# Root and rows of the norm on GpSimd, statistics in other units, and four of six low parts on VectorE, in a kernel of linear attention and experts

## The reference

```python
xn = layernorm(x)
# attention: 16 heads of 16, 128 random features a head
q, k, v = split(xn @ W_qkv.T)
q_p = elu(q @ proj) + 1 ; k_p = elu(k @ proj) + 1
kv = k_p.T @ v
attn = (q_p @ kv) / (q_p @ k_p.sum(tokens) + 1e-8)
# experts: 8 of 256 -> 1024 -> 256, the two best of each token
logits = xn @ Wr + br ; weights = softmax over the top 2
ffn = sum_e weights_e * (gelu(xn @ W1_e + b1_e) @ W2_e + b2_e)
out = x + attn @ W_out.T + b_out + ffn
```

## Time and profile before

| | us |
|---|---|
| median of three runs | 700.1 |
| profiled execution | 700.86 |
| its span, first to last instruction | 698.7 |
| TensorE busy | 682.9 |
| VectorE busy | 504.1 |
| ScalarE busy | 475.3 |
| GpSimd busy | 227.9 |

### The profile page before, as it was taken

How to read it: one execution, slowest core, us unless ns; L and a number is a source line. 1 busy time by engine, 2 the same in 40 slices (tenths; PEclk the granted TensorE clock), 3 DMA queues, 4 the chain that set the end, 5 groups by cost and what they waited for, 6 DMA issues and landing times.

```text
span 698.7 us, 17362 instructions
## 1 busy us (share of the span) xinstructions
PE 682.9 (98%) x5503; PEld 603.3 (86%) x5504; DVE 504.1 (72%) x1246; ACT 475.3 (68%) x875; POOL 227.9 (33%) x169
## 2 busy tenths in 40 slices
PE   8899999999999998999999999999999999999996
PEld 4666777777777776589999999999999999999996
DVE  8798888888888878748577675556777545577544
ACT  5687969696969696776557775447775444577553
POOL 2053232323232324643232532225233222322422
PEclk9999999999999999999999999999999999999999
DMA  8856474747474647765455663336556333454531
GB/s 266 200 182 170 108 228 106 228 106 228 106 228 106 198 106 223 224 189 142 100 98 118 145 167 46 46 47 106 178 71 167 48 52 53 81 131 107 69 48 23
DMA packets 87205, 91.65 MB, mean 131 GB/s; under 512 B 60049, under 2 KB 73361, under 8 KB 84897
## 3 DMA queue, kind: packets, MB, share of 16 engines
q1 hardware_dynamic: 71426, 59.36, 33.9%
q0 software_dynamic: 13872, 18.75, 15.2%
q10 hardware_dynamic: 1872, 13.11, 5.1%
HBM read 39.32 MB, written 26.67 MB: 94 GB/s over the span
## 4 chain that ended last, share of the span: by engine, by line
PE 82%; DVE 6%; issue 4%; ACT 2%; POOL 2%; DMA 2%; SPq 1%; POOLq 0%; DVEq 0%
PE F L527 9%; PE F L528 9%; PE F L529 9%; PE WK L527 5%; PE F L596 5%; PE WK L529 4%; PE WK L528 4%; PE NUM L527 4%; PE NUM L529 4%; PE NUM L528 4%; PE DEN L605 4%; PE DEN L527 4%; PE DEN L529 4%; PE DEN L528 4%; PE F L590 3%
## 5 line engine op out<-in xcount | busy, mean ns | idle before, releaser
L1932 POOL DMA_INDIRECT out<-ysb,icur x75 | 121.0, 1613 | 270.6 <-DVE ysb L1763 241.0
L1218 ACT ACTIVATE h<-F,b1c 128x384 f32<-128x384 f32 x200 | 112.2, 575 | 140.0 <-PE F L529 131.2
L1740 DVE TENSOR_TENSOR hl<-h,hh 128x768 fp32r<-128x768 f32 x100 | 96.1, 962 | 111.6 <-ACT hh L1222 111.6
L1063 ACT ACTIVATE e_ring<-F 128x512 f32<-128x512 f32 x256 | 145.7, 621 | 38.5 <-PE F L590 35.0
L527 PE MATMUL F<-gxh,wh 128*128 128x384 f32 (+1 forms) x400 | 128.6, 321 | 0.4 <-DVE wl L1641 0.4
L528 PE MATMUL F<-gxl,wh 128*128 128x384 f32 (+1 forms) x400 | 128.0, 320 | 0.0
L529 PE MATMUL F<-gxh,wl 128*128 128x384 f32 (+1 forms) x400 | 128.0, 320 | 0.0
L1866 POOL DMA_INDIRECT xg<-rows,slots x64 | 63.2, 988 | 174.0 <-PE F L590 158.8
L1468 DVE SCALAR_TENSOR_TENSOR kp<-F,e_ring 128x512 f32<-128x512 f32 x128 | 82.7, 680 | 13.2 <-PE DEN L605 6.2
L1468 DVE SCALAR_TENSOR_TENSOR qp<-F,e_ring 128x512 f32<-128x512 f32 x128 | 85.2, 683 | 8.5 <-ACT e_ring L1063 7.0
L1222 ACT ACTIVATE hh<-h 128x768 fp32r<-128x768 f32 x100 | 84.6, 846 | 3.3
(11 more groups left out here) (261 smaller groups left out, 1552.6 us busy)
## 6 DMA issues: line engine op xcount, KB each, us to landing
wraw<-experts ACTq DMA_DIRECT2D x12, 1024.0 KB, 6.2
gblk<-xg SPq DMA_DIRECT2D x100, 96.0 KB
Sk<-kdh SPq DMA_DIRECT2D x64, 128.0 KB, 2.3
Sq<-qdh SPq DMA_DIRECT2D x64, 128.0 KB
xin<-x SPq DMA_DIRECT2D x8, 512.0 KB, 5.5
Sk<-kdl SPq DMA_DIRECT2D x32, 128.0 KB, 2.4
Sq<-qdl SPq DMA_DIRECT2D x32, 128.0 KB
xres<-x SPq DMA_DIRECT2D x8, 512.0 KB
```

Of the source, the lines that this page charges most:

```text
L1063: A(e_ring[:, u % 4, :], F[u % 4][:, :], ACT.Exp, bias=EXP_BIAS, scale=1.0 / DOWN).then_inc(exp_done, 1)
L1218: A(h32[:, m, :], F[m % 4][:, 0:T], ACT.Gelu, bias=b1c[:, w, m:m + 1]).then_inc(gelu, 1)
L1740: V.tensor_tensor(hl[:, 2 * q:2 * q + 2, :], h32[:, 2 * q:2 * q + 2, :], f32(hh[:, 2 * q:2 * q + 2, :]), ALU.subtract).then_inc(hl_rdy, 1)
L1932: pool.indirect_dma_start(out, bass.IndirectOffsetOnAxis(icur[:, s, :], 0), ysb[:, s, :], None, bounds_check=last_token, compute_op=ALU.ad ...
```

## The change

- *Root and rows.* VectorE makes statistics, variance and seed. From batch 2 on GpSimd computes the inverse root (`norm_root`: eleven `tensor_tensor` on 128x4 elements, each waiting for the one before) and writes `xn` (`norm_rows`: four `tensor_scalar`). They stand behind the sends: root of batch `b + 2`, copy of the rows of `b + 1`, rows of `xn` for `b + 2`, and then the bias.
- *Next tokens.* SyncE's `load_x(b + 3)` stands between `stack_k(b + 1)` and `stack_q(b + 1)`.
- *Statistics.* From pass 2 on they stand in units 1 and 2 and the variance with the seed in unit 8; in passes 0 and 1 (`late`) they stay in 16 and 17, and variance and seed are together in 18.
- *Low parts.* `qk_rest` and `qk_lo` of groups 0, 1, 2 and `heads_rest` and `at_lo` of group 0 are gone in the loop. VectorE subtracts the high part from the bank instead: `qk_low` ahead of features 12, 17 and 23, `heads_low` ahead of feature 22. Groups 3 and 1 stay as they were, and so does the last batch's end.

```diff
@@ sync
+        load_x(3)
+        with sp.Fori(1, NB - 3) as b:
+            stack_k(b + 1)
+            load_x(b + 3)
+            stack_q(b + 1)
+            store_o(b - 1)
+            load_xres(b)
...
@@ tensor, iteration
                 if u == 11:
                     kv(b, 1)
-                    qk_rest(b + 1, 0)
...
-                if u == 18:
-                    qk_rest(b + 1, 1)
...
                 if u == 21:
-                    if not first:
-                        heads_rest(b - 1, 0)
                     v_logits(b + 1, 1)
                 if u == 23:
-                    qk_rest(b + 1, 2)
                     pe.wait_ge(kv_rdy, b + 1)
                     v_logits(b + 1, 2)
...
@@ scalar, iteration
-                if u == 11:
-                    qk_lo(b + 1, 0)
...
                 if u == 19:
-                    qk_lo(b + 1, 1)
                     v_copy(b + 1, 0)
...
-                    if not first:
-                        at_lo(b - 1, 0)
-                if u == 22:
-                    qk_lo(b + 1, 2)
...
@@ vector
+        def qk_low(b, i):
+
+            dve.wait_ge(qkh_rdy, 4 * b + i + 1)
+            high, low = ((kdh, kdl), (qdh, qdl))[i // 2]
+            V.tensor_tensor(low[:, i % 2, :], QK_BANK[i][:, :], f32(high[:, i % 2, :]), ALU.subtract).then_inc(qkl_rdy, 1)
+
+        def heads_low(b):
+
+            dve.wait_ge(ath_rdy, 2 * b + 1)
+            V.tensor_tensor(atl[:, 0, :], AT_BANK[0][:, :], f32(ath[:, 0, :]), ALU.subtract).then_inc(atl_rdy, 1)
...
-        def iteration(b, first=False, ahead=True):
+        def iteration(b, first=False, ahead=True, late=False):
             for u in range(32):
-                if u == 0 and not first:
-                    norm_rows(b + 1, 0, 4)
+                if ahead and u == (16 if late else 1):
+                    norm_stats(b + 2, 0, 2)
+                if ahead and u == (17 if late else 2):
+                    norm_stats(b + 2, 2, 4)
+                    join()
+                if ahead and u == (18 if late else 8):
+                    norm_var(b + 2)
+                    for i in range(SEED_STEPS):
+                        norm_step(b + 2, i)
...
+                if u == 12:
+                    qk_low(b + 1, 0)
+                if u == 17:
+                    qk_low(b + 1, 1)
+                if u == 22 and not first:
+                    heads_low(b - 1)
+                if u == 23:
+                    qk_low(b + 1, 2)
...
@@ gpsimd
+        def norm_root(b, i):
...
+            pool.wait_ge(seed_rdy, i + 1)
+            G.tensor_tensor(rtmp[:, 0, :], seed, seed, ALU.mult).then_inc(root_step, 1)
+            pool.wait_ge(root_step, ROOT_STEPS * i + 1)
+            G.tensor_tensor(rtmp[:, 1, :], rtmp[:, 0, :], var[:, :], ALU.mult).then_inc(root_step, 1)
...
+        def norm_rows(b, i):
+            pool.wait_ge(root_step, ROOT_STEPS * i + 11)
+            pool.wait_ge(rows_rdy, b)
+            pool.wait_ge(xT_full, KT * b)
+            pool.sem_inc(root_rdy, 1)
+            for n in range(NT):
+                last = nc.gpsimd.tensor_scalar(xn[:, n, :], xin[:, n, :], mv[:, n, 0:1], rs[:, 1, n:n + 1], ALU.subtract, ALU.mult)
+            last.then_inc(xn_rdy, 1)
...
-        with pool.Fori(1, NB - 1) as b:
+        with pool.Fori(1, NB - 2) as b:
             send(b)
+            norm_root(b + 2, b)
+            copy_rows(b + 1)
+            norm_rows(b + 2, b)
             add_bias(b - 1)
-            copy_rows(b + 1)
```

More of the change, by code:

```diff
@@ L53 @@
 C_T, C_LIM, C_OFF = 324, 336, 344
-C_END = C_OFF + E * TT
+C_ROOT = C_OFF + E * TT
+C_END = C_ROOT + 4
+CUBE = 0.375
 def constants():
@@ L245, in build @@
     xn_first = sem("xn_first")
+    seed_rdy = sem("seed_rdy")
+    root_step = sem("root_step")
+    root_rdy = sem("root_rdy")
     xT_full = sem("xT_full")
@@ L320, in build @@
     ROUTE_STEPS = 8
-    NORM_STEPS, CUBE = 9, 0.375
-    STEPS_AT = {19: (0, 1), 21: (2,), 23: (3, 4), 24: (5,), 25: (6,), 26: (7,), 29: (8,)}
+    NORM_STEPS = 9
+    SEED_STEPS, ROOT_STEPS = 2, 11
     PIECES, PIECE = 4, 1024
@@ L437, in _ @@
         stack_q(1)
-        with sp.Fori(1, NB - 2) as b:
-            load_x(b + 2)
+        load_x(3)
[5 more added lines that the diff above has]
+            load_xres(b)
+        for b in (NB - 3, NB - 2):
             stack_k(b + 1)
@@ L443, in _ @@
             load_xres(b)
[L444 to L447, removed]
         load_raw = load_raw_on(sp)
@@ L1040, in qk_lo @@
         def qk_lo(b, i):
-            act.wait_ge(qkr_full, 4 * b + i + 1)
+            act.wait_ge(qkr_full, i + 1 if isinstance(b, int) and b == 0 else 4 + b)
             A((kdl, qdl)[i // 2][:, i % 2, :], QK_BANK[i][:, :], ACT.Copy).then_inc(qkl_rdy, 1)
@@ L1364, in norm_step @@
             elif i == 1:
-                link(V.tensor_scalar(seed.bitcast(I32), var[:, :].bitcast(I32), -0.5, float(0x5F3759DF), ALU.mult, ALU.add))
+                guess = V.tensor_scalar(seed.bitcast(I32), var[:, :].bitcast(I32), -0.5, float(0x5F3759DF), ALU.mult, ALU.add)
+                if isinstance(b, int) and b < 2:
+                    link(guess)
+                else:
+                    guess.then_inc(seed_rdy, 1)
             elif i == 2:
@@ L1726, in _ @@
         before = chain[1] + ROUTE_STEPS
-        iteration(0, first=True)
+        iteration(0, first=True, late=True)
         batch_steps = chain[1] - before
-        with dve.Fori(1, NB - 2) as b:
+        iteration(1, late=True)
+        with dve.Fori(2, NB - 2) as b:
             chain[:] = before + b * batch_steps, 0
@@ L1860, in copy_rows, with constant @@
             nc.gpsimd.tensor_copy(rows[:, :, 0:D], xn[:, :, :]).then_inc(rows_rdy, 1)
+        def norm_root(b, i):
+            G = nc.gpsimd
+            seed, cubic, root = rs[:, 1, :], rs[:, 0, :], rs[:, 1, :]
+            def constant(k):
+                return cst[:, C_ROOT + k:C_ROOT + k + 1].to_broadcast([P, NT])
+            pool.wait_ge(seed_rdy, i + 1)
+            G.tensor_tensor(rtmp[:, 0, :], seed, seed, ALU.mult).then_inc(root_step, 1)
+            pool.wait_ge(root_step, ROOT_STEPS * i + 1)
+            G.tensor_tensor(rtmp[:, 1, :], rtmp[:, 0, :], var[:, :], ALU.mult).then_inc(root_step, 1)
+            pool.wait_ge(root_step, ROOT_STEPS * i + 2)
+            G.tensor_tensor(rtmp[:, 0, :], rtmp[:, 1, :], constant(0), ALU.add).then_inc(root_step, 1)
+            pool.wait_ge(root_step, ROOT_STEPS * i + 3)
+            G.tensor_tensor(rtmp[:, 0, :], rtmp[:, 0, :], rtmp[:, 1, :], ALU.mult).then_inc(root_step, 1)
+            pool.wait_ge(root_step, ROOT_STEPS * i + 4)
+            G.tensor_tensor(rtmp[:, 0, :], rtmp[:, 0, :], constant(1), ALU.add).then_inc(root_step, 1)
+            pool.wait_ge(root_step, ROOT_STEPS * i + 5)
+            G.tensor_tensor(cubic, rtmp[:, 0, :], seed, ALU.mult).then_inc(root_step, 1)
+            pool.wait_ge(root_step, ROOT_STEPS * i + 6)
+            G.tensor_tensor(rtmp[:, 0, :], cubic, cubic, ALU.mult).then_inc(root_step, 1)
+            pool.wait_ge(root_step, ROOT_STEPS * i + 7)
+            G.tensor_tensor(rtmp[:, 1, :], rtmp[:, 0, :], var[:, :], ALU.mult).then_inc(root_step, 1)
+            pool.wait_ge(root_step, ROOT_STEPS * i + 8)
+            G.tensor_tensor(rtmp[:, 0, :], rtmp[:, 1, :], constant(2), ALU.mult).then_inc(root_step, 1)
+            pool.wait_ge(root_step, ROOT_STEPS * i + 9)
+            G.tensor_tensor(rtmp[:, 0, :], rtmp[:, 0, :], constant(3), ALU.add).then_inc(root_step, 1)
+            pool.wait_ge(root_step, ROOT_STEPS * i + 10)
+            G.tensor_tensor(root, rtmp[:, 0, :], cubic, ALU.mult).then_inc(root_step, 1)
@@ L1891, in _ @@
         send(0)
+        norm_root(2, 0)
         copy_rows(1)
-        with pool.Fori(1, NB - 1) as b:
+        norm_rows(2, 0)
+        with pool.Fori(1, NB - 2) as b:
             send(b)
+            norm_root(b + 2, b)
+            copy_rows(b + 1)
+            norm_rows(b + 2, b)
             add_bias(b - 1)
-            copy_rows(b + 1)
+        send(NB - 2)
+        add_bias(NB - 3)
+        copy_rows(NB - 1)
         def split_weights(c):
```

3 lines of the change are left out of this document (2 added, 1 removed).

## The result

The changed kernel takes 704.19 us, the median of five runs (703.19 to 705.06), beside 700.08 (699.58 to 700.13) for the kernel before: a ratio of 1.0054, interval 1.0042 to 1.0065. Its profiled execution took 704.36 us, 702.5 of it span. The forecast was 704.1 us and slower.

The account below looks back on a forecast made before the run. TensorE looked like the bound, but its weight loads of units 26 and 27 already waited for VectorE, so places there decide. Batch 0, batch 1 and the rest, 1.1 + 1.4 + 1.55 = 4.0 us, gave 704.1 us, range 696.9 to 706.5.

Parts of the forecast that it names:

- Units 0 to 11, nothing: Middle pass: moved statistics, and aggregate, variance and seed (0.75 us) before feature 8, lie in VectorE's waits and cost nothing.
- Unit 17, 0.12 late: Middle pass: the first removed matmul gives nothing, and unit 17's weight load waits for VectorE, 0.12 us late.
- Units 18 to 21, 0.12 early: Middle pass: qk_low(1) ends early, the second removed matmul gives its 0.24 us, unit 21 is 0.12 early.
- The row of five on VectorE from feature 21: Middle pass: features 21 to 23 with two subtractions between run back to back; unit 27 and the pass are 0.31 us late.
- Batches 2 to 6: The middle passes, each 0.31 us late: 1.55 us in all.
- Batch 1: Statistics stay late, ahead of qk_low(1): to_heads starts 1.0 us late and unit 27 is 1.4 us late.
- Batch 0: Three new qk_low subtractions, less removed steps and idle time on VectorE, make it 1.1 us longer.
- GpSimd hidden: GpSimd after its sends: root steps, copy, rows and bias take 7.8 of the 15.3 us before the residual needs the bias.
- The lock: SBUF port, locked for a whole instruction: GpSimd's new work can meet only VectorE's short two-input routing steps; no cost added.
- Rival (a), the matmuls pay: If feature 23 starts no later in the pass, TensorE keeps its saving, 6.3 us: 693.8 us; chance 0.25.
- (b): Both effects cancel: late batches milder, half the removed matmuls paid, 698.7 to 701.5 us; chance 0.13.
- (c): GpSimd's chain too long: at 0.98 us a step the residual waits, 8 us on top, 712 us; chance 0.07.

Follow-up runs that it names:

- exp. 2: Kernel before with only the four VectorE subtractions replacing the minus matmuls; root, rows and statistics stay as before: 710.87 us, ratio 1.0141.
- exp. 3: Changed kernel with heads_low one unit earlier (ahead of feature 21) and qk_low(2) one unit later (ahead of feature 24): 698.01 us, ratio 0.996 to the kernel before.
- exp. 4: Changed kernel with qk_low(0) ahead of feature 8, variance and seed ahead of feature 14: 701.93 us, ratio 1.0016 to the kernel before.
- the first experiment: Changed kernel with the norm part alone, all six low parts as in the kernel before: 700.12 us, ratio 0.9988 to the kernel before.
- experiment 12: Changed kernel, subtractions ahead of features 8, 21, 24, seed ahead of 14, qk_low(1) earlier in passes 0 and 1: 715.96 us, before 719.79 on that chip.
- experiment 7: Changed kernel with GpSimd's norm_rows taking two constants instead of per-partition values from batch 2 on: 723.87 us in one run, on a slower chip.
- 11: Kernel before, unchanged, profiled on a chip of the slower kind: 720.85 us in one run, 719.79 the median there.

## Why the prediction was right

Places in batch 3, us from the pass's first exponential, read from the timelines (a dash: not drawn):

| | before | predicted | after | exp. 2 | exp. 3 | exp. 4 |
|---|---|---|---|---|---|---|
| unit 17 | 15.28 | 15.39 | 15.40 | 15.37 | 15.41 | 15.04 |
| unit 21 | 20.75 | 20.63 | 20.75 | 21.79 | 20.74 | 20.41 |
| exponential 21 | 21.92 | 21.32 | 21.44 | 22.48 | 21.43 | 21.10 |
| feature 21 | 22.56 | 21.96 | 22.06 | 23.11 | 22.06 | 21.72 |
| feature 23 | 24.05 | 24.36 | 24.47 | 25.81 | 23.38 | 24.13 |
| unit 26 | 23.90 | 23.90 | 24.00 | 25.05 | 23.51 | 23.67 |
| unit 27 | 24.80 | 25.10 | 25.20 | 26.54 | 24.20 | 24.86 |
| pass | 35.02 | 35.33 | 35.43 | 36.78 | 34.43 | 35.09 |

- *Units 0 to 11, nothing.* Right. Aggregate, variance and seed took 0.96 us ahead of feature 8 instead of 0.75, and feature 8 starts at 10.63 for 10.61; the first experiment has the pass unchanged.
- *Unit 17, 0.12 late.* Right, 0.12.
- *Units 18 to 21, 0.12 early.* Wrong by 0.12: unit 21 stands where it stood. Behind the waiting unit 17, `kv(2)` follows 0.42 us after it instead of 0.32 (in experiment 4, where unit 17 doesn't wait, 0.33). A weight load that has to wait doesn't lie under the matmul ahead of it: unit 17's matmul takes 0.49 us instead of 0.39. The prediction charged the wait but not that tenth. It is the mis-sized term: everything from unit 21 on is 0.10 to 0.12 later than drawn, and that is the whole difference between 0.31 and 0.41 a pass.
- *The row of five on VectorE from feature 21.* Right in every link: 0.60 a link, and exponential 21 0.48 earlier in the pass instead of 0.60.
- *Batches 2 to 6.* 2.16 us instead of 1.55, by that term: five times 0.1 and a bit.
- *Batch 1.* Predicted 1.4, with `to_heads` 1.0 late; measured 1.44, unit 20 to unit 21 1.01 longer, and TensorE's wait names the subtraction. VectorE and TensorE of batch 1 (first exponential at 54.10):

```profile
73.83 0.69 DVE L1401 TENSOR_TENSOR kdl<-WK,kdh 128x512 fp32r<-128x512 f32 x1
```

```profile
74.57 0.66 PE L648 MATMUL WK<-cst,at 128*128 128x128 f32 x4 [0.83 <-DVE kdl L1401]
```

- *Batch 0.* Predicted 1.1, measured 0.8 to 1.0 by the two pairs of equal clock.
- *Sum.* The parts are 4.4 to 4.6 us, the medians differ by 4.1, 4.0 was predicted. The middle passes were taken 0.6 too low and batch 0 some 0.2 too high, and start and experts scatter by as much. The match to 0.1 us is luck; the match to 0.5 isn't.
- *GpSimd hidden.* Right, with a wrong number inside. Steps 0.28 for 0.3; the four rows 4.84 for 1.06 with an upper bound of 2.41. Root to bias is 11.6 us instead of 7.8 and still ends 4.5 ahead of the residual. The bound was drawn from a copy and a two-tensor operation of the same size, on the assumption that a third kind must lie between; it doesn't. The GPSIMD Engine Reference of the Trainium skill (4.1 Engine selection) led the same way, one-input operations at about line rate; the 4.84 us beside the copy's 1.04 contradict it here, and the measurement decides.
- *The lock.* SBUF — State Buffer of the Trainium skill (Who interferes with whom) was used for GpSimd meeting only short VectorE instructions, and their being held up was put at nothing. That is the step the prediction had wrong at no cost. The bias, pushed back by the new work, holds up `lg` by 0.7 us a pass in after (0.89 for 0.18), which agrees with a lock for the whole instruction; TensorE doesn't wait for it at the places of the change. With better places it does, 0.42 us a pass in experiment 12. The rows hold VectorE up far less: `lg` beside them takes 0.18 us (batch 1 of after), and a small instruction that started within 0.2 us of a row's start took 0.45 to 0.50 instead of 0.18 (`cumb` at 82.79 in after, for one). In the other direction nothing is seen: the eleven steps take 0.20 to 0.22 us each, and experiment 7's rows 1,061 to 1,093 ns over 24 instructions.
- *Rival (a), the matmuls pay.* It named its own condition, feature 23 before 24.05. The change misses it by 0.42 and loses; experiment 3 meets it (23.38) and gains 0.59 of the 0.94 us a pass. The rival was a true one: two unit numbers decide between it and the forecast.
- *Rivals (b) and (c)* fell: the time lies outside what (b) allows, and the residual doesn't wait for GpSimd.

## What to carry to other kernels

When two engines are nearly full, a moved instruction costs by its place: find the feature or tile that the bound engine waits for, follow the queue back to the last idle gap, and put the work ahead of that gap's end or behind the awaited instruction. Two of the four subtractions, each shifted by one unit, made the difference between a pass 0.41 us longer than before and one 0.59 shorter. And bound an unseen operation on another engine by more than its neighbours' prices, or be sure that the cover holds several times the bound, as it did here for the residual. Ask also what the new work pushes back on its own engine, and what that will then run beside: here a bias addition, moved by 9 us, held up a small VectorE instruction, which cost nothing until the better places made TensorE wait for it.

## What the runs showed of the hardware

- GpSimd: chained steps on 128x4 take 0.20 us each and 0.28 from start to start. A `tensor_scalar` with subtract and mult on 128x256 takes 1.21 us with per-partition values (4.84 for four) and 1.06 with constants, while a copy of four times as many columns takes 1.04.
- While GpSimd added two SBUF tensors of 128x1024 (2.40 us), a VectorE addition of two SBUF tensors of 128x32 didn't finish: it took 0.19 to 1.98 us by where GpSimd's stood, and always ended 0.05 us after it (44 passes of eleven kernels). Alone it takes 0.18. Beside GpSimd's copy of 1,024 columns one small VectorE instruction took 1.04 us instead of 0.18 (`mskb` at 49.67 in after).
- A weight load that waited for a semaphore set its successor back by 0.10 us more than the wait (units 16 to 18 in batch 3).
- TensorE's granted clock fell to 0.50 for 3.4 us early in batch 0 in some executions (before, experiments 2, 3, 4 and 11, from about 27 us on) and not in others (after, experiment 1). Ahead of it TensorE was busy 5.26 of 7.00 us in before and 5.23 of 7.00 in experiment 1, which kept its clock, so its work doesn't tell the two apart. The price is about 0.7 us: batch 0 took 33.46 in before and 32.72 in experiment 1.
- On some chips the dense small matmuls of `kv` come in pieces with pauses of 0.4 to 0.7 us, in the unchanged kernel too: 1.7 us a middle pass and 9.5 in batch 0, part of it from a mean clock of 0.84 there.
